# One of VectorE's score rows computed by GpSimd in 84 of 128 attention blocks

## The chip, the core and the metric

The kernel runs on one core of a Trainium2 chip. The metric is the device time of one execution in microseconds (us). Of the engines, PE is TensorE, DVE is VectorE, ACT is ScalarE, POOL is GpSimd and SP is the queue that issues the transfers.

## What is computed

Eight graphs of 2048 nodes with 128 features go through four layers. Each layer is a residual sum and a layer norm. Layers 0, 2 and 3 multiply by a normalised adjacency matrix and a weight. Layer 1 is an attention whose score is not a plain product:

```python
# layers 0, 2, 3 (with small differences in the degree)
x = layernorm(x + (D^-1/2 (adj + I) D^-1/2 x) W + b)
# layer 1, per graph, i and j over 2048 nodes, d over 128 features
q = x @ WQ
k = x @ WK
h = relu(q[:, None, :, :] + k[:, :, None, :])
score = einsum('bijd,d->bij', h, p)
att = softmax(score + mask)           # mask: 0 where adj > 0, else -1e22
x = layernorm(x + att @ x)
```

The array `h` has 2048 x 2048 x 128 elements for each graph, and making it is most of the work.

## The kernel before

**Blocks and rows.** The attention of a graph is cut into 16 blocks (`t` from 0 to 15) of 128 nodes i; eight graphs give 128 blocks. In a block the 128 nodes are walked as 32 groups (`g`) of 4 rows (`u`). One row is one instruction over a 128 x 2048 tile (features by nodes j) for one node i: it takes `q` and the column of `k` that belongs to i. Of the 32 groups, 20 are DVE's (kind "D", L990, a max of two packed half-precision numbers read as one float) and 12 are ACT's (kind "A", L756, a relu). The groups g = 2, 5, 7, 10, 13, 15, 18, 21, 23, 26, 29, 31 are ACT's.

**Rings.** The rows of a group lie in `big`. Each kind has a ring of two groups (`RING = 2`), so DVE may write its group number r only when PE has used up group r - 2 (`rows_used["D"]`). In one block DVE's groups are g = 0, 1, 3, 4, 6, and so on, so group 4 goes into the place of group 1, and group 3 into that of group 0.

**PE.** For each group PE runs `score_rows` (L1134): it multiplies the rows by a window of weights, 32 matmuls for a D group, into the four banks of `score`. It takes the groups in the order of g, whoever made them. Between groups it does its other work (`side`): transposes of adjacency tiles (L1034), products of the graph layers (L1057, L1075), the attention product (L1116).

**Side work.** The layers 0, 2 and 3 of other graphs run beside the attention, each in four steps. Step s of layer2 has its block 2 + s, of layer3 its block 6 + s, of layer0 its block 10 + s (`BLOCK`). Every engine walks the same list of places (32 for a block), and `side` says what stands at a place. The sum of a step (`sum_layer`, place 35 of its step) falls on g = 3 of the block behind: DVE runs four products with sum that read PSUM (L871), four BN_STATS (L877) and four BN_AGGR (L883), and after that its rows of g = 3. POOL's `layer_root` (L587, L589) stands at g = 4, and `norm_layer` (L890), which uses its result, at g = 8. The sums fall on blocks 3 to 14; the first attention has layer0 alone (4 sums), six have all twelve, the last one has eight: 84 blocks in all. Twelve more sums lie outside the attention.

**Softmax.** The scores of the block before are read by DVE (`masked_scores`, L941, L945) between row u = 1 and row u = 2 of g = 1 (in block 0 at g = 0).

**Order.** All of it is written out by hand: each engine's instructions stand in program order, with semaphores between the engines. `load_k` and `load_q` on SP bring the columns of `k` and the tiles of `q` for later rows and wait until the rows that read the old ones are done.

Of the kernel before, what the change touches and what calls it, by code (L numbers as in the profile page):

```python
# [9 lines left out]
ALU = mybir.AluOpType  # L10
# [20 lines left out]
def build(nc, x, adj, w0, b0, wq, wk, p, w2, b2, w3, b3, out):  # L31
# [50 lines left out]
    with ExitStack() as ctx:  # L82
# [3 lines left out]
        def sem(name):  # L86
            return ctx.enter_context(nc.semaphore(name))
# [134 lines left out]
        att_variance_ready = sem("att_variance_ready")  # L222
        att_rstd_ready = sem("att_rstd_ready")
        att_output = sem("att_output")

        block = ctx.enter_context(nc.Block())

# [5 lines left out]

        def masked_at(t):
            return (0, 0) if t == 0 else (1, 2)

# [3 lines left out]
        def one_of(c, *which):  # L242
            return c in which

        def block_of(c, t):
            return c * T + (T + t)
# [8 lines left out]
        def step_of(c, name, s):  # L255
            return layer_of(c, name) * STEPS + s
# [104 lines left out]
        def _(sp):  # L361
# [43 lines left out]
            def load_k(c, t):  # L405
                sp.wait_ge(k_stored, qk_step(c + 1, t // PER) * 16 + 16)
                sp.wait_ge(pair_stored, split_of(c + 1, t // PER, 1) * 16 + 16)
                n = block_of(c, t)
                if not one_of(c, FIRST) or t > 1:
                    for kind in "AD":  # L410
                        sp.wait_ge(rows_ready[kind], (c * T + (T + t - 1)) * N_OF[kind])
                sp.dma_start(k_cols[:, t % 2, :], k_kept[n]).then_inc(k_loaded[t % 2], 16)
                sp.dma_start(k_pair_cols[:, t % 2, :], k_pair_kept[n]).then_inc(k_loaded[t % 2], 16)

# [103 lines left out]
            def load_q(c):  # L518
                sp.wait_ge(q_stored, qk_step(c + 1, STEPS) * 16)
                sp.wait_ge(pair_stored, split_of(c + 1, STEPS, 0) * 16)  # L520
                if not one_of(c, FIRST):
                    sp.wait_ge(rows_ready["A"], (c + 1) * (T * N_OF["A"]))
                sp.dma_start(q_f32[:], q_kept[c + 1]).then_inc(q_loaded, 16)
                if not one_of(c, FIRST):
                    sp.wait_ge(rows_ready["D"], (c + 1) * (T * N_OF["D"]))
                sp.dma_start(q_pair[:], q_pair_kept[c + 1]).then_inc(q_pair_loaded, 16)

            def attention(c):
# [45 lines left out]
        @block.gpsimd  # L574
        def _(pool):
            pool.memset(ident[:], 0.0).then_inc(ident_cleared, 1)
            pool.wait_ge(ident_cleared, 1)
            pool.affine_select(out=ident[:], in_=ident[:], compare_op=ALU.not_equal, fill=1.0, base=0,
                               pattern=[[-1, P]], channel_multiplier=1).then_inc(ident_ready, 1)
            pool.wait_ge(minus_half_ready, 1)  # L580
            pool.wait_ge(bound_ready, 2)
            pool.tensor_tensor(bound, bound2, plus_half, ALU.pow).then_inc(bound_ready, 1)

            def layer_root(c, name, s):
                n = step_of(c, name, s) + 1
                pool.wait_ge(moments_ready, n)
                pool.tensor_scalar(var_eps[:], moments[:, :, 1], EPS, None, ALU.add).then_inc(variance_ready, 1)  # L587
                pool.wait_ge(variance_ready, n)
                pool.tensor_tensor(rstd[:], var_eps[:], minus_half[:, 0:PER], ALU.pow).then_inc(rstd_ready, 1)  # L589

            def att_root(m):
                pool.wait_ge(att_moments_ready, m + 1)
                pool.tensor_scalar(att_var[:], att_mom[:, 1:2], EPS, None, ALU.add).then_inc(att_variance_ready, 1)  # L593
                pool.wait_ge(att_variance_ready, m + 1)
                pool.tensor_tensor(att_rstd[:], att_var[:], minus_half[:, 0:1], ALU.pow).then_inc(att_rstd_ready, 1)

            def hold_roots(c):
                pool.wait_ge(roots_ready, roots_before(c))
                pool.tensor_copy(dis_hold[:], dis_new[:, 1:3, :]).then_inc(roots_ready, 1)

            def degree_roots(c):
                pool.wait_ge(degrees_ready, c + 3)
                if not one_of(c, OPENING):
                    pool.wait_ge(roots_ready, roots_before(c) + 1)
                for i in range(3):
                    pool.tensor_tensor(dis_new[:, i, :], deg_sum[:, i, :], minus_half[:], ALU.pow).then_inc(roots_ready, 1)

            def keep_roots(c):
                pool.wait_ge(roots_ready, roots_before(c) + (1 if one_of(c, LAST) else 4))
                pool.tensor_copy(dis_use[:], dis_hold[:]).then_inc(roots_ready, 1)  # L610

            def side(c, place):
                for name, s in steps_at(c, place, ROOT_AT):
                    layer_root(c, name, s)
                if place == DIS_AT:
                    if not one_of(c, OPENING, CLOSING):
                        hold_roots(c)
                    if not one_of(c, LAST, CLOSING):
                        degree_roots(c)
                if place == KEEP_AT and not one_of(c, OPENING, CLOSING):  # L620
                    keep_roots(c)

            def attention(c):
                for place in range(PLACES):
                    t, g = divmod(place, GROUPS)
                    if g == NORM_AT and (t > 0 or not one_of(c, FIRST)):
                        att_root(c * T + (T + t - 1))
                    side(c, place)

            for place in range(PLACES):  # L630
                side(OPENING, place)
            attention(FIRST)
            for c in range(B - 2):
                attention(c)
            attention(LAST)
            att_root(B * T - 1)
            for place in range(PLACES):
                side(CLOSING, place)
# [137 lines left out]
        def _(dve):  # L776
# [88 lines left out]
            def sum_layer(c, name, s):  # L865
                n = step_of(c, name, s) + 1
                dve.wait_ge(biased, n)
                dve.wait_ge(layer_projected, n)
                for j in range(PER):
                    t = s * PER + j  # L870
                    ins = nc.vector.scalar_tensor_tensor(out=gx[:, t, :], in0=acc[0][:, j * P:(j + 1) * P],  # L871
                                                         scalar=dis[name][:, t:t + 1], in1=gx[:, t, :],
                                                         op0=ALU.mult, op1=ALU.add)
                ins.then_inc(layer_summed, 1)
                dve.wait_ge(layer_summed, n)
                for j in range(PER):
                    ins = nc.vector.bn_stats(stats[:, j, :], gx[:, s * PER + j, :])  # L877
                ins.then_inc(stats_ready, 1)
                dve.wait_ge(stats_ready, n)
                if n > 1:  # L880
                    dve.wait_ge(layer_output, n - 1)
                for j in range(PER):
                    ins = nc.vector.bn_aggr(moments[:, j, :], stats[:, j, :])  # L883
                ins.then_inc(moments_ready, 1)
# [81 lines left out]
            def attention(c):  # L966
                for place in range(PLACES):
# [12 lines left out]
                    if KIND[g] == "D":  # L980
                        if RANK[g] == 0:
                            if t == 0:
                                dve.wait_ge(q_pair_loaded, (c + 2) * 16)
                            dve.wait_ge(k_loaded[t % 2], (c + 1) * (T // 2 * 32) + (t // 2 * 32 + 32))
                        dve.wait_ge(rows_used["D"], n * N_OF["D"] + (RANK[g] + 1))
                        for u in range(P // QUAD):
                            if before and u > 0 and (g, u) == masked_at(t):
                                masked_scores(n)

                            ins = nc.vector.tensor_scalar(ring["D"][:, RANK[g] % RING * 4 + u, :], q_pair[:],  # L990
                                                          k_pair_cols[:, t % 2, QUAD * u + g:QUAD * u + g + 1],
                                                          None, ALU.max)
                        ins.then_inc(rows_ready["D"], 1)
# [17 lines left out]
        def _(pe):  # L1011
# [106 lines left out]
                if cc == CHUNKS - 1:  # L1118
                    ins.then_inc(acc_full, 1)

            def score_rows(n, g):
                kind = KIND[g]
                pe.wait_ge(rows_ready[kind], n * N_OF[kind] + (RANK[g] + 1))
                window = unit_window if kind == "D" else sign_window
                for cc in range(CHUNKS):
# [17 lines left out]
            def attention(c):  # L1143
                for place in range(PLACES):
# [9 lines left out]
                            pe.wait_ge(x1_ready, (c + 2) * 16)  # L1154
                        weigh(m, MULTIPLY_AT[g], steps_turned(c, place))
                    side(c, place)
                    score_rows(block_of(c, t), g)

            for u in range(UNITS):
                first_unit(u)  # L1160
# [41 lines left out]
```

## Time and profile before

| what | value |
|---|---|
| median of 3 runs | 14251.69 us (14249.84 to 14259.41) |
| the profiled execution, its own time | 14255.09 us |
| its span, first to last instruction | 14253.3 us |
| PE busy | 13023.6 us (91%) |
| DVE busy | 13509.2 us (95%) |
| ACT busy | 13092.2 us (92%) |
| POOL busy | 668.9 us (5%) |
| mean granted TensorE clock | 0.982 of full speed |

Three engines are nearly full, and POOL is nearly empty. A busy share is an average: which engine holds up the others changes several times within a block, so the place of the change has to be read in the order of time. The granted clock has two levels here, full (2.4 GHz) and half (1.2 GHz).

### The profile page before, as it was taken

What the parts mean: (1) busy time and instruction counts of PE and PEld (TensorE: products, weight loads), DVE (VectorE), ACT (ScalarE), POOL (GpSimd) and SP (SyncE); (2) the same over time, 40 slices, a digit from 0 to 9 for tenths busy, and PEclk for the clock granted to TensorE, in tenths of its full rate; (3) what the DMA queues carried; (4) which work ended last, traced back from release to release, by engine and by line L of the source; (5) the groups of instructions that cost most, each with busy time, mean ns of one, the idle gap of its engine ahead of it and who ended that gap; (6) DMA issues with size and microseconds to landing.
All of it is one profiled execution on the core that took longest, in us unless ns stands there. A gap on an engine that the chain in (4) does not pass through costs nothing.

```text
span 14253.3 us, 317325 instructions
## 1 busy us (share of the span) xinstructions
PE 13023.6 (91%) x143877; PEld 5459.3 (38%) x143877; DVE 13509.2 (95%) x14168; ACT 13092.2 (92%) x8612; POOL 668.9 (5%) x495
## 2 busy tenths in 40 slices
PE   6889989999899988999989998899989999899988
PEld 3333334443344333443334433344333433333333
DVE  5999999999999999999999999999999999999995
ACT  5999899998999899998999989999899998998994
POOL 0000000000000000000000000000000000000000
PEclk7999999999999999999999999999999999999999
DMA  5111112221122111221122211222112221011103
GB/s 184 45 51 47 49 52 86 85 61 50 55 86 87 62 40 63 87 87 56 36 72 84 86 56 36 75 84 85 56 35 75 88 78 56 30 49 51 42 12 108
DMA packets 714328, 935.44 MB, mean 66 GB/s; under 512 B 61713, under 2 KB 455953, under 8 KB 693521
## 3 DMA queue, kind: packets, MB, share of 16 engines
q1 hardware_dynamic: 712976, 915.13, 20.5%
q8 instruction: 1128, 18.48, 0.5%
q14 instruction: 224, 1.83, 0.0%
HBM read 722.01 MB, written 184.55 MB: 64 GB/s over the span
## 4 chain that ended last, share of the span: by engine, by line
PE 45%; DVE 35%; ACT 16%; issue 2%; DMA 2%; SPq 0%; POOL 0%; ACTq 0%; DVEq 0%; POOLq 0%
PE score L1134 33%; DVE big L990 31%; ACT big L756 14%; PE acc L1057 6%; PE turn L1034 2%; PE acc L1116 2%; DVE att L941 2%; DVE gx L871 1%; DMA piece<-adj_turned 1%; DMA big<-in_adj_dram 0%; ACT y_turned L679 0%; DVE stats L877 0%; ACT turned L669 0%; DMA q_pair_kept<-turned 0%; PE acc L1075 0%
## 5 line engine op out<-in xcount | busy, mean ns | idle before, releaser
L990 DVE TENSOR_SCALAR big<-q_pair,k_pair_cols 128x2048 f32<-128x2048 f32 x10240 | 12366.6, 1281 | 380.0 <-PE score L1134 362.6
L756 ACT ACTIVATE big<-q_f,k_cols 128x2048 f32<-128x2048 f32 x6144 | 11746.9, 1999 | 70.2 <-DMA q_f<-q_kept 44.1
L1134 PE MATMUL score<-big,unit_window 128*32 128x512 f16 x81920 | 5178.8, 396 | 819.0 <-DVE big L990 788.4
L1134 PE MATMUL score<-big,sign_window 128*32 128x512 f32 x49152 | 5619.7, 597 | 273.2 <-ACT big L756 268.6
L1134 PEld LDWEIGHTS score<-big,unit_window 128*32 128x32 bf16 x81920 | 2270.4, 96 | 4003.1 <-DVE big L990 1242.9
L1134 PEld LDWEIGHTS score<-big,sign_window 128*32 128x32 f32 x49152 | 1569.0, 110 | 3603.8 <-issue 3005.9
L1057 PE MATMUL acc<-piece,gs 128*128 128x512 f32 x3072 | 1446.6, 598 | 36.0 <-DMA piece<-adj_turned 23.6
L1057 PEld LDWEIGHTS acc<-piece,gs 128*128 128x128 f32 x3072 | 533.8, 191 | 545.4 <-issue 459.1
L737 ACT ACTIVATE att_turned<-turn 128x512 f32<-128x512 f32 x512 | 300.9, 588 | 390.5 <-PE turn L1034 389.7
L593 POOL TENSOR_SCALAR att_var<-att_mom 128x1 f32<-128x1 f32 x128 | 66.0, 515 | 10641.0 <-DVE att_mom L959 10641.0
L1116 PE MATMUL acc<-x,att_turned 128*128 128x128 f32 x4096 | 554.9, 279 | 0.0
L693 ACT ACTIVATE y_turned<-acc 128x512 f32<-128x512 f32 x96 | 57.7, 601 | 523.4 <-PE acc L1057 522.8
L1116 PEld LDWEIGHTS acc<-x,att_turned 128*128 128x128 f32 x4096 | 498.3, 192 | 56.8 <-issue 56.8
L941 DVE CUSTOM_DVE_ANT_0 att<-score,att 128x512 f32<-128x512 f32 x512 | 324.7, 687 | 42.1 <-PE score L1134 41.6
L1034 PEld LDWEIGHTS turn<-ident,att 128*128 128x128 f32 x2048 | 215.2, 141 | 331.9 <-issue 327.0
L1034 PE MATMUL turn<-ident,att 128*128 128x128 f32 x2048 | 336.5, 287 | 3.8 <-ACT att L733 3.1
L1034 PE MATMUL turn<-ident,raw 128*128 128x128 f32 x1792 | 277.0, 277 | 29.0 <-DMA raw<-in_adj_dram 29.0
L669 ACT ACTIVATE turned<-turn 128x512 f32<-128x512 f32 x448 | 262.1, 585 | 34.4 <-PE turn L1034 34.4
L733 ACT ACTIVATE att<-att,neg_max 128x2048 f32<-128x2048 f32 x128 | 256.0, 2000 | 20.4 <-DVE neg_max L945 19.9
L1034 PEld LDWEIGHTS turn<-ident,raw 128*128 128x128 f32 x1792 | 203.9, 141 | 120.1 <-issue 84.1
L682 ACT ACTIVATE y_turned<-raw 128x1024 bf16<-128x1024 f32 x224 | 237.1, 1058 | 7.1
L587 POOL TENSOR_SCALAR var_eps<-moments 128x4 f32<-128x4 f32 x96 | 110.6, 1152 | 2699.7 <-DVE moments L883 2699.7
(88 smaller groups left out, 2592.0 us busy)
## 6 DMA issues: line engine op xcount, KB each, us to landing
piece<-adj_turned SPq DMA_DIRECT2D x1536, 256.0 KB, 2.8
att<-in_adj_dram SPq DMA_DIRECT2D x128, 1024.0 KB, 5.1
raw<-in_adj_dram SPq DMA_DIRECT2D x224, 512.0 KB, 4.6
adj_turned<-turned SPq DMA_DIRECT2D x224, 512.0 KB, 4.3
big<-in_adj_dram SPq DMA_DIRECT2D x32, 512.0 KB, 7.6
adj_turned<-big SPq DMA_DIRECT2D x32, 512.0 KB, 6.9
gx<-in_x_dram SPq DMA_DIRECT2D x32, 256.0 KB, 4.2
q_kept<-raw SPq DMA_DIRECT2D x32, 256.0 KB, 3.4
```

Source lines behind the costliest of these rows:

```text
L669: nc.scalar.activation(stage[:, k * BANK:(k + 1) * BANK], turn[1][:], ACT.Copy).then_inc(turn_free[1], 1)
L682: nc.scalar.activation(unread, raw[:], ACT.Abs, accum_out=abs_part[:, u % 2, u // 2:u // 2 + 1]).then_inc(raw_abs_summed, 1)
L733: nc.scalar.activation(att[:], att[:], ACT.Exp, bias=neg_max[:], accum_out=row_sum[:]).then_inc(exp_ready, 1)
L737: nc.scalar.activation(att_turned[:, cc % 2, :], turn[0][:], ACT.Copy).then_inc(turn_free[0], 1)
L756: ins = nc.scalar.activation(ring["A"][:, RANK[g] % RING * 4 + u, :], q_f32[:], ACT.Relu, bias=k_cols[:, t % 2, QUAD * u + g:QUAD * u + g ...
L871: ins = nc.vector.scalar_tensor_tensor(out=gx[:, t, :], in0=acc[0][:, j * P:(j + 1) * P], scalar=dis[name][:, t:t + 1], in1=gx[:, t, :], o ...
L941: nc.vector.tensor_tensor_reduce(out=part, in0=score[:, cc, :], in1=part, scale=1.0, scalar=-3.0e38, op0=ALU.add, op1=ALU.max, accum_out=b ...
L990: ins = nc.vector.tensor_scalar(ring["D"][:, RANK[g] % RING * 4 + u, :], q_pair[:], k_pair_cols[:, t % 2, QUAD * u + g:QUAD * u + g + 1], ...
L1034: ins = nc.tensor.transpose(turn[k][:, j * P:(j + 1) * P], src(j), ident[:])
L1057: nc.tensor.matmul(acc[1][:], gs[:, i, :], piece[:, i % PIECES, :], start=(i == 0), stop=(i == T - 1)) \
L1116: ins = nc.tensor.matmul(acc[0][:, 0:D], att_turned[:, cc % 2, j * P:(j + 1) * P], x1[:, cc * PER + j, :], start=(cc == 0 and j == 0), sto ...
L1134: ins = nc.tensor.matmul(score[QUAD * u:QUAD * (u + 1), cc, :], window[:, QUAD - 1 - g:2 * QUAD - 1 - g], row, start=(g == 0 and part == 0 ...
```

## The change

In each of the 84 blocks, row u = 3 of group g = 4 is taken from DVE's list and put on POOL's. POOL computes it with an instruction of two operations: a min with 3.0e38, which alters no value that occurs, and then the same max. POOL waits for four things: a new semaphore `pool_may_go`, which the first of the four products of that sum raises; `q` and `k` in place; and `rows_used["D"]`, the same count that DVE waits for before its own rows of g = 4. In POOL's order the row stands ahead of `layer_root` of the same sum. PE waits in `score_rows` for `pool_row_ready` beside `rows_ready`, and SP's `load_k` and `load_q` wait for it too.

```diff
+        POOL_ROW = (4, 3)
+
+        def sums_at(c, t):
+            return [(name, s) for name in side_layers(c) for s in range(STEPS) if BLOCK[name] + s + 1 == t]
+
+        def has_pool_row(c, t):
+            return len(sums_at(c, t)) > 0
+
+        def pool_rows(c, t):
+            return sum(has_pool_row(a, k) for a in range(FIRST, c + 1) for k in range(T) if a < c or k < t)
...
@@ load_k, SP
+                    done = pool_rows(c, t - 1) if t > 0 else pool_rows(c - 1, T - 1)
+                    if done > 0:
+                        sp.wait_ge(pool_row_ready, done)
...
@@ load_q, SP
+                    sp.wait_ge(pool_row_ready, pool_rows(c, 0))
...
@@ POOL
+            def row(c, t):
+                g, u = POOL_ROW
+                n = block_of(c, t)
+                for name, s in sums_at(c, t):
+                    pool.wait_ge(pool_may_go, step_of(c, name, s) + 1)
+                pool.wait_ge(q_pair_loaded, (c + 2) * 16)
+                pool.wait_ge(k_loaded[t % 2], (c + 1) * (T // 2 * 32) + (t // 2 * 32 + 32))
+                pool.wait_ge(rows_used["D"], n * N_OF["D"] + (RANK[g] + 1))
+                pool.tensor_scalar(ring["D"][:, RANK[g] % RING * 4 + u, :], q_pair[:], 3.0e38,
+                                   k_pair_cols[:, t % 2, QUAD * u + g:QUAD * u + g + 1], ALU.min, ALU.max) \
+                    .then_inc(pool_row_ready, 1)
...
+                    if g == POOL_ROW[0] and has_pool_row(c, t):
+                        row(c, t)
...
@@ sum_layer, DVE
                 for j in range(PER):
                     t = s * PER + j
+                    if j == 1:
+                        ins.then_inc(pool_may_go, 1)
...
@@ attention, DVE
+                            if (g, u) == POOL_ROW and has_pool_row(c, t):
+                                continue
...
@@ PE
-            def score_rows(n, g):
-                kind = KIND[g]
+            def score_rows(c, t, g):
+                kind, n = KIND[g], block_of(c, t)
+                if g == POOL_ROW[0] and has_pool_row(c, t):
+                    pe.wait_ge(pool_row_ready, pool_rows(c, t) + 1)
                 pe.wait_ge(rows_ready[kind], n * N_OF[kind] + (RANK[g] + 1))
```

The rows of DVE's program around one such sum, in the kernel before. L871, L877 and L883 are the sum, L990 a row of scores, L890 the norm of the step.

```order
L945 TENSOR_REDUCE neg_max<-bank_max 128x1 [waits scores_read]
L990 TENSOR_SCALAR big<-q_pair,k_pair_cols 128x2048 x2
L871 SCALAR_TENSOR_TENSOR gx<-acc,dis_use,gx 128x128 [waits layer_projected,biased]
L871 SCALAR_TENSOR_TENSOR gx<-acc,dis_use,gx 128x128 x3
L877 BN_STATS stats<-gx 128x6 [waits layer_summed]
L877 BN_STATS stats<-gx 128x6 x3
L883 BN_AGGR moments<-stats 128x2 [waits layer_output,stats_ready]
L883 BN_AGGR moments<-stats 128x2 x3
L990 TENSOR_SCALAR big<-q_pair,k_pair_cols 128x2048 [waits vector_rows_used]
L990 TENSOR_SCALAR big<-q_pair,k_pair_cols 128x2048 x3
L990 TENSOR_SCALAR big<-q_pair,k_pair_cols 128x2048 [waits vector_rows_used]
L990 TENSOR_SCALAR big<-q_pair,k_pair_cols 128x2048 x3
```

The same place in the changed kernel, where L905, L911 and L917 are the sum and L1026 a row of scores.

```order
L905 SCALAR_TENSOR_TENSOR gx<-acc,dis_use,gx 128x128 [waits layer_projected,biased]
L905 SCALAR_TENSOR_TENSOR gx<-acc,dis_use,gx 128x128 x3
L911 BN_STATS stats<-gx 128x6 [waits layer_summed]
L911 BN_STATS stats<-gx 128x6 x3
L917 BN_AGGR moments<-stats 128x2 [waits layer_output,stats_ready]
L917 BN_AGGR moments<-stats 128x2 x3
L1026 TENSOR_SCALAR big<-q_pair,k_pair_cols 128x2048 [waits vector_rows_used]
L1026 TENSOR_SCALAR big<-q_pair,k_pair_cols 128x2048 x3
L1026 TENSOR_SCALAR big<-q_pair,k_pair_cols 128x2048 [waits vector_rows_used]
L1026 TENSOR_SCALAR big<-q_pair,k_pair_cols 128x2048 x2
```

Group g = 3 keeps its four rows, and group g = 4 has three. POOL's program there, in the changed kernel: L623 is the row, L605 and L607 the root of the step (L587 and L589 before), L611 and L613 the root of the attention.

```order
L613 TENSOR_TENSOR att_rstd<-att_var,minus_half 128x1 [waits att_variance_ready]
L623 TENSOR_SCALAR big<-q_pair,k_pair_cols 128x2048 [waits k1_loaded,vector_rows_used,q_pair_loaded,pool_may_go]
L605 TENSOR_SCALAR var_eps<-moments 128x4 [waits moments_ready]
L607 TENSOR_TENSOR rstd<-var_eps,minus_half 128x4 [waits variance_ready]
L611 TENSOR_SCALAR att_var<-att_mom 128x1 [waits att_moments_ready]
```

The row stands between the two roots, and it is the only instruction that POOL gains in a block.

## Rows read from the trace of the kernel before

**Rows 1.** The page: busy time of each engine, and the chain that ended last.

```profile
PE 13023.6 (91%) x143877; PEld 5459.3 (38%) x143877; DVE 13509.2 (95%) x14168; ACT 13092.2 (92%) x8612; POOL 668.9 (5%) x495
...
PE 45%; DVE 35%; ACT 16%; issue 2%; DMA 2%; SPq 0%; POOL 0%; ACTq 0%; DVEq 0%; POOLq 0%
```

**Rows 2.** The chain around one sum: start us, us, what.

```profile
5974.18 2.47 DVE big L990 x2
5976.65 1.05 DVE gx L871 x4
...
5978.63 0.38 DVE moments L883 x4
5979.01 9.55 DVE big L990 x8
5988.56 0.04 issue
5988.60 5.42 PE score L1134 x55
```

**Rows 3.** DVE in time there: start us, us, engine line op, operands, count.

```profile
5976.57 1.12 DVE L871 SCALAR_TENSOR_TENSOR gx<-acc,dis_use,gx 128x128 f32<-128x128 f32 x4
5977.72 0.87 DVE L877 BATCH_NORM_STATS2 stats<-gx 128x6 f32<-128x128 f32 x4
5978.63 0.38 DVE L883 BATCH_NORM_AGGREGATE moments<-stats 128x2 f32<-128x6 f32 x4
5978.93 14.41 DVE L990 TENSOR_SCALAR big<-q_pair,k_pair_cols 128x2048 f32<-128x2048 f32 x12
```

**Rows 4.** PE in time there: the groups 0 and 1, 2, 3 and 4.

```profile
5975.62 3.82 PE L1134 MATMUL score<-big,unit_window 128*32 128x512 f16 x64
5979.26 3.62 PE L1134 MATMUL score<-big,sign_window 128*32 128x512 f32 x32
5983.82 2.00 PE L1134 MATMUL score<-big,unit_window 128*32 128x512 f16 x32 [0.95 <-DVE big L990]
5988.60 1.99 PE L1134 MATMUL score<-big,unit_window 128*32 128x512 f16 x32 [2.78 <-DVE big L990]
```

**Rows 5.** PE in time, another such block: groups 1, 2, 3 and 4.

```profile
5115.80 2.02 PE L1134 MATMUL score<-big,unit_window 128*32 128x512 f16 x32 [1.95 <-DVE big L990]
5117.63 3.62 PE L1134 MATMUL score<-big,sign_window 128*32 128x512 f32 x32
5122.91 1.99 PE L1134 MATMUL score<-big,unit_window 128*32 128x512 f16 x32 [1.66 <-DVE big L990]
```

**Rows 6.** DVE's rows by their line: duration ns min/median/max.

```profile
L990 DVE TENSOR_SCALAR big<-q_pair,k_pair_cols x10240: 1251/1281/1307, 235.8 to 14065.5; 128x2048 f32<-128x2048 f32 x197
```

**Rows 7.** POOL in time: beside DVE's rows, and where DVE has none.

```profile
5979.10 1.18 POOL L587 TENSOR_SCALAR var_eps<-moments 128x4 f32<-128x4 f32 x1 [29.47 <-DVE moments L883]
5980.35 2.26 POOL L589 TENSOR_TENSOR rstd<-var_eps,minus_half 128x4 f32<-128x4 f32 x1
...
165.70 0.23 POOL L587 TENSOR_SCALAR var_eps<-moments 128x4 f32<-128x4 f32 x1 [28.18 <-DVE moments L883]
166.01 1.03 POOL L589 TENSOR_TENSOR rstd<-var_eps,minus_half 128x4 f32<-128x4 f32 x1
```

**Rows 8.** POOL by line and form: busy us, mean ns of one, idle before.

```profile
L578 POOL TENSOR_SCALAR_AFFINE_SELECT ident<-ident 128x128 f32<-128x128 f32 x1 | 0.3, 294 | 0.2 <-POOL ident L576 0.2
L576 POOL MEMSET ident<- 128x128 f32 x1 | 0.2, 206 | 0.3 <-POOLq L1189 0.3
L1189 POOL MEMSET const-float32-1.0<- 128x1 f32 x1 | 0.1, 100 | 0.0
```

**Rows 9.** TensorE's clock (PEclk, behind POOL) behind the idle time, two blocks.

```profile
4465.30:4468.70 3.40, 3.28 (x32) 1.27 (x36) 3.40 (x4) 3.40 (x2) 0.00 (x0) 0.50 0.00 0
6207.40:6210.80 3.40, 3.28 (x48) 1.40 (x52) 3.40 (x4) 3.40 (x2) 0.00 (x0) 1.00 0.00 0
```

**Rows 10.** PE's group 4 at half clock (first, last, and the block of rows 9), and at full.

```profile
1416.47 3.01 PE L1134 MATMUL score<-big,unit_window 128*32 128x512 f16 x32 [2.79 <-DVE big L990]
...
4465.42 3.51 PE L1134 MATMUL score<-big,unit_window 128*32 128x512 f16 x32 [2.78 <-DVE big L990]
...
6207.52 2.00 PE L1134 MATMUL score<-big,unit_window 128*32 128x512 f16 x32 [2.78 <-DVE big L990]
...
13373.62 3.24 PE L1134 MATMUL score<-big,unit_window 128*32 128x512 f16 x32 [2.80 <-DVE big L990]
```

**Rows 11.** The first product of this and of the next sum, for the same two blocks.

```profile
4453.38 1.12 DVE L871 SCALAR_TENSOR_TENSOR gx<-acc,dis_use,gx 128x128 f32<-128x128 f32 x4
...
4563.53 1.12 DVE L871 SCALAR_TENSOR_TENSOR gx<-acc,dis_use,gx 128x128 f32<-128x128 f32 x4
...
6195.49 1.12 DVE L871 SCALAR_TENSOR_TENSOR gx<-acc,dis_use,gx 128x128 f32<-128x128 f32 x4
...
6304.25 1.12 DVE L871 SCALAR_TENSOR_TENSOR gx<-acc,dis_use,gx 128x128 f32<-128x128 f32 x4
```

More of the change, by code:

```diff
@@ L224, in build @@
         att_output = sem("att_output")
+        pool_row_ready = sem("pool_row_ready")
+        pool_may_go = sem("pool_may_go")
         block = ctx.enter_context(nc.Block())
@@ L1156, in attention @@
                     side(c, place)
-                    score_rows(block_of(c, t), g)
+                    score_rows(c, t, g)
             for u in range(UNITS):
```

## Prediction, made before the changed kernel was run

> **What bounds the kernel now.** I read the page first, then the chain of waits around one sum, then the timelines of DVE, PE and POOL there, and last the granted clock. The page shows three engines above 90% and POOL at 5%, and a chain that is PE for 45%, DVE for 35% and ACT for 16% [rows 1]. So the bound changes hands within a block, and only the chain tells who holds it at the place of the change. There it is DVE, without a break: the last two rows of group 1, the sum, then eight rows (groups 3 and 4), and then PE takes over with group 4 [rows 2]. PE stands idle 0.95 us before group 3 and 2.78 us before group 4, both times for DVE [rows 4]. The pattern is the same in all 84 blocks with a sum: the first product of the sum is on the chain, DVE's rows begin 2.36 us behind its start, and PE begins group 4 at 12.04 us (5976.57 to 5988.60 in [rows 3, 4]). So a microsecond that DVE gains or loses between the sum and group 4 moves PE's group 4, and the chain goes on from there.
>
> **What the change removes.** One row of the eight. Rows follow each other every (14.41 - 1.28) / 11 = 1.19 us [rows 3, 6]. 84 x 1.19 = 100 us come off the chain, if nothing comes on.
>
> **When POOL's row can begin.** The words of the change say behind the first product, which is 0.3 us into the sum. But the row goes into the ring place of group 1, and POOL also waits until PE has used that group. PE is not that far. In the block of [rows 4] groups 0 and 1 end at 5979.44, which is 2.87 us behind the start of the sum. In the block of [rows 5], where PE is early, group 1 ends at 5117.82, with the sum begun 7.25 us before PE's group 3 at 5122.91, hence at 5115.66: 2.16 us. I find the early kind in 35 of the 84 blocks (2.14 to 2.20 us) and the late kind in 49 (2.4 to 2.96 us). DVE begins its rows at 2.36 us. So the cover of the sum is gone when POOL gets the go: in the early kind POOL starts about 0.09 us behind PE (the delay of var_eps behind the last BN_AGGR: 5979.01 to 5979.10 in [rows 2, 7]), just ahead of DVE, and in the late kind DVE's first row is already running.
>
> **What happens when the two meet.** POOL's small instructions show one side. var_eps takes 0.23 us alone and 1.18 us when it is issued in the middle of a DVE row; it ends with that row. The root takes 1.03 us alone and 2.26 us beside rows [rows 7]. So POOL waits for the row that runs, and gets in between two rows although DVE has the next one ready. DVE shows nothing of it: its longest row in 10240 is 1307 ns [rows 6]. But these POOL instructions touch 1 to 16 elements a partition. No row of this trace has a long POOL instruction, so what DVE pays must be bounded. I take the same exclusion to hold in the other direction: DVE's next row waits for POOL's whole row.
>
> The Trainium skill says so too ("SBUF — State Buffer", Who interferes with whom): whichever of a DVE instruction in a two-port mode and a GpSimd instruction comes first holds the shared ports for its whole length and the other blocks fully, and tensor_scalar can be in such a mode while a product that reads PSUM is not. The trace agrees for POOL's side (0.23 against 1.18 us); no row of it shows DVE's side. By that rule the place behind the first product would be right, if the ring let POOL use it.
>
> **How long POOL's row takes.** Alone, a POOL tensor_scalar of 4 elements takes 0.23 us [rows 7]. The slope per element is bounded by the two instructions that have 128 elements: memset, (206 - 100) / 127 = 0.83 ns, and affine_select, at most (294 - 100) / 128 = 1.5 ns [rows 8]. With 2048 elements the row is 0.2 + 1.7 = 1.9 us or 0.2 + 3.1 = 3.3 us. I take the lower slope: an estimate from memset's row, since affine_select has its own fixed cost in its 294 ns. In the early kind DVE loses 2.16 + 0.09 + 1.9 - 2.36 = 1.8 us; in the late kind the fixed part lies beside DVE's first row and DVE loses 1.7 us and two hand-overs of about 0.1 us. I take 1.9 us for both. Bounds: 0 (DVE isn't held at all) and 3.3 us.
>
> "GPSIMD Engine Reference", 3.1, of the Trainium skill gives 1.03 cycles an element at 1.2 GHz for bodies of up to two operations, which would be an estimate of 1.76 us for the elements; no run here shows it yet.
>
> **The term of DVE's path.** (1.9 - 1.19) x 84 = 60 us slower. The bounds make it -100 and (3.3 - 1.19) x 84 = +177 us.
>
> **TensorE's clock.** Behind the 2.78 us of idle time before group 4 the granted clock is at its lower level (1.2 GHz) in some blocks: 0.50 for 3.4 us in the block at 4465 and 1.00 in the one at 6207 [rows 9]. Group 4 then takes 3.51 us where it takes 2.00 us [rows 10]. By the duration of group 4 this is so in 42 of the 84 blocks (first and last in [rows 10]). None of the 84 has a slow group 3, which has 0.9 to 1.7 us of idle time before it [rows 4, 5]. What it costs a block is the time to the next sum: 110.15 us against 108.76 us [rows 11], 1.4 us; other pairs that I compared lie between 0 and 1.5 us, so I take 1.0, and 42 us in all.
> The change shifts the idle time. Group 3 is ready later by what DVE loses, 1.9 us: PE waits 2.8 to 3.6 us before group 3. Group 4 follows three rows later, 3.6 us, of which PE works 2.0: it waits 1.6 us there. A wait of up to 1.7 us was never followed by the lower clock, so I expect the low stretches to move to group 3. There they cost little, since a group 3 of 3.5 us (as group 4 in [rows 10]) still ends before group 4's rows are ready at 3.6 us. I leave 12 us for stretches that reach into group 4. The term is 12 - 42 = -30 us, with bounds -50 (all of the cost gone) and +42 (both places slow).
>
> **Other parts.** POOL's roots come later by about 3 us; rstd ends at 5982.61 [rows 7], and the norm stands behind the twelve rows of DVE that last to 5993.3 [rows 3], so 0. PE's added wait holds up only group 4, and POOL is done some 5 us before DVE's third row of it: 0; if POOL came later than that, everything behind it in PE's order would wait. SP waits for rows that are done a block earlier: 0.
>
> **Sum.** 60 - 30 = +30 us on the profiled execution's 14255.1 us. That execution is 3.4 us above the median of the runs shown, and I put the difference on the median: 14251.7 + 30 = 14282 us. A change under 0.2% (28 us) can't be told from none in a measurement of this kernel, so this forecast lies just beyond that.
>
> **Rivals.**
> - *Faster: DVE is not held.* POOL reads and writes between DVE's accesses, or DVE is held only a little. For it: DVE's rows don't lengthen beside POOL's small instructions [rows 6, 7]. Against it: POOL is held by DVE, so something is shared. DVE gains 1.19 x 84 = 100 us; PE's wait before group 4 falls to 1.6 us, so the 42 us of the clock go too. ACT at 92% would take some of it back. 14252 - 100 - 42 = 14110 us at best; 14130 to 14200 where DVE is held for half a row. It decides below 0.9 us of loss. Chance 0.22.
> - *No change: the loss is 1.5 to 1.9 us and the clock gives back 45 us or more.* Memset's slope without hand-overs gives 1.7: (1.7 - 1.19) x 84 = 43 us, less 45. 14250 us, up to 14275. Chance 0.28.
> - *Much slower: POOL's row has affine_select's slope.* 3.3 us: 14252 + 177 - 42 + 12 = 14399 us. Two operations instead of one and a scalar read from memory speak for it; that affine_select builds a pattern as well speaks against it. Chance 0.12.
> - *Starved: POOL doesn't get in until DVE's run of rows ends.* In [rows 3] the run is 14.41 us long; PE would wait for the row from 12 to about 19 us, some 7 us in each of 84 blocks, 590 us. var_eps, which gets in within 1.18 us, speaks against it. Chance 0.03.
>
> **How the numbers follow.** My forecast (slower by 28 to 90 us) has 0.35; with the two slower rivals (0.12 and 0.03) the chance of slower is 0.50, of no change 0.28, of faster 0.22. The forecast's own range is 14262 to 14340 us. For 8 in 10 I go down to 14185, where half a row's hold still lies, and up to 14390, near affine_select's slope; the full gain and the starved case stay outside.
>
> **What would show it.** In the changed kernel POOL's row (L623) should start 2.2 to 2.3 us behind the first product in some blocks and 2.5 to 3.0 us in the others, never at 0.4. DVE should show a hole or one long row of 1.7 to 2.0 us in g = 3. PE's wait before group 3 should be 2.8 us or more and before group 4 about 1.6 us, with the lower clock at group 3 and full clock at group 4. POOL's row should be done in 1.9 to 3 us. The prediction is wrong if DVE's rows keep their 1.19 us beside POOL's row, if the row lasts over 2.5 us, or if the lower clock comes as often at group 4 as before.

## The result, and the profile after

| kernel | median us | runs | against the kernel before, with its 95% interval |
|---|---|---|---|
| before | 14252.8 | 11 | |
| changed | 14295.4 | 11 | 1.0035 [1.0019, 1.0051] |

The change costs 42.6 us. One of its eleven runs took 14409.0 us at a mean granted clock of 0.944, where the others had 0.976 to 0.979; without it the median is 14291.1 us. The profiled execution of the changed kernel took 14306.2 us, 11 us above its median, so single blocks are compared below rather than the two spans.

The page of the changed kernel, engines first and then its chain. DVE is busier by 35 us although it has 84 instructions less, and POOL by 298 us (compare [rows 1]).

```profile
PE 13055.2 (91%) x143877; PEld 5481.5 (38%) x143877; DVE 13544.5 (95%) x14084; ACT 13092.1 (92%) x8612; POOL 967.3 (7%) x579
...
PE 42%; DVE 35%; ACT 18%; issue 2%; DMA 2%; SPq 0%; POOL 0%; ACTq 0%; DVEq 0%; POOLq 0%
```

The chain around the sum of the same block as in [rows 2] (start us, us, what).

```profile
5988.81 2.47 DVE big L1026 x2
5991.28 1.05 DVE gx L905 x4
...
5993.26 0.38 DVE moments L917 x4
5993.64 10.00 DVE big L1026 x7
6003.63 0.14 issue
6003.77 5.45 PE score L1172 x62
```

Seven rows take 10.00 us where eight took 9.55 us, and PE starts 0.14 us behind the last of them instead of 0.04 us, now that it waits for two semaphores there. In the mean of the 84 blocks PE's group 4 begins 12.57 us behind the sum's start; it was 12.04 us.

POOL in time there.

```profile
5994.31 3.44 POOL L623 TENSOR_SCALAR big<-q_pair,k_pair_cols 128x2048 f32<-128x2048 f32 x1 [30.05 <-PE score L1172]
5997.73 1.20 POOL L605 TENSOR_SCALAR var_eps<-moments 128x4 f32<-128x4 f32 x1
5999.01 2.26 POOL L607 TENSOR_TENSOR rstd<-var_eps,minus_half 128x4 f32<-128x4 f32 x1
```

What released the row is PE's score, not DVE's product, and the row starts 3.12 us behind the sum's start (5991.19). The DVE row that was running at 5997 us, and the line's extremes (min/median/max in ns; compare [rows 6]):

```profile
5995.92 2.92 DVE L1026 TENSOR_SCALAR big<-q_pair,k_pair_cols 128x2048 f32<-128x2048 f32 x1
...
L1026 DVE TENSOR_SCALAR big<-q_pair,k_pair_cols x10156: 1251/1280/2926, 237.2 to 14117.5; 128x2048 f32<-128x2048 f32 x200
```

One row, the third of group 3, lasts 2.92 instead of 1.28 us. The 1.64 us more are what POOL's row costs DVE; below they are called the hold. Each of the 84 blocks has one such row of 2.91 to 2.93 us: the third of group 3 in 82 blocks, the fourth in two.

PE in time (groups 0 and 1, 2, 3, 4), which answers to [rows 4].

```profile
5990.25 3.85 PE L1172 MATMUL score<-big,unit_window 128*32 128x512 f16 x64
5993.91 3.63 PE L1172 MATMUL score<-big,sign_window 128*32 128x512 f32 x32
6000.09 2.00 PE L1172 MATMUL score<-big,unit_window 128*32 128x512 f16 x32 [2.55 <-DVE big L1026]
6003.77 2.01 PE L1172 MATMUL score<-big,unit_window 128*32 128x512 f16 x32 [1.68 <-DVE big L1026]
```

PE now waits 2.55 us before group 3 (0.95 before) and 1.68 us before group 4 (2.78 before).

### The profile page after: what moved, and what is told of

Its sections match the earlier page's. It is cut to its first block, busy times and chain, and to the rows that moved or that the text cites. A ratio compares the mean times of both kernels' runs of the same rounds, so it can differ in the third digit from the quotient of the medians.

```text
span 14304.4 us, 317584 instructions
## 1 busy us (share of the span) xinstructions
PE 13055.2 (91%) x143877; PEld 5481.5 (38%) x143877; DVE 13544.5 (95%) x14084; ACT 13092.1 (92%) x8612; POOL 967.3 (7%) x579
## 4 chain that ended last, share of the span: by engine, by line
PE 42%; DVE 35%; ACT 18%; issue 2%; DMA 2%; SPq 0%; POOL 0%; ACTq 0%; DVEq 0%; POOLq 0%
DVE big L1026 31%; PE score L1172 31%; ACT big L788 16%; PE acc L1093 6%; PE turn L1070 2%; PE acc L1152 2%; DVE att L975 2%; DVE gx L905 1%; DMA piece<-adj_turned 1%; ACT y_turned L711 0%; ACT turned L701 0%; DMA q_pair_kept<-turned 0%; DVE stats L911 0%; DMA big<-in_adj_dram 0%; PE acc L1111 0%
## 5 line engine op out<-in xcount | busy, mean ns | idle before, releaser
L1026 DVE TENSOR_SCALAR big<-q_pair,k_pair_cols 128x2048 f32<-128x2048 f32 x10156 | 12401.1, 1293 | 394.6 <-PE score L1172 373.5
L611 POOL TENSOR_SCALAR att_var<-att_mom 128x1 f32<-128x1 f32 x128 | 65.3, 511 | 10379.2 <-DVE att_mom L993 10379.2
L623 POOL TENSOR_SCALAR big<-q_pair,k_pair_cols 128x2048 f32<-128x2048 f32 x84 | 311.5, 3708 | 2488.8 <-PE score L1172 2488.8
```

Source lines behind the costliest of these rows:

```text
L623: pool.tensor_scalar(ring["D"][:, RANK[g] % RING * 4 + u, :], q_pair[:], 3.0e38, k_pair_cols[:, t % 2, QUAD * u + g:QUAD * u + g + 1], ALU ...
```

## Experiments

Each kernel is the changed one with the edit shown, if nothing else is said. The cover is work of DVE beside which POOL's row can run without holding DVE; early and late blocks are those of the prediction (35 and 49 of the 84). Every median stands beside runs of the kernel before on the same chip (14254.7 to 14257.2 us).

**Where the row lies.**

```diff
-        POOL_ROW = (4, 3)
+        POOL_ROW = (3, 3)
```

> POOL's row is moved from (g 4, u 3) to (g 3, u 3), with the same wait on the first product; its ring place is that of group 0, which PE has used up 0.1 to 0.9 us behind the start of the sum. Theory A (the ring count of group 1 let POOL start only when the cover of the sum was gone, and DVE then stands still for POOL's elements): POOL starts 0.4 to 1.0 us behind the first product, its 1.7 us of elements lie mostly beside the sum, DVE's hole of 1.64 us shrinks to 0 to 0.6 us, PE's group 3 and 4 come 0.6 to 1.2 us earlier than in the kernel before; 14252 - 84 x 0.6 to 1.2 = 14150 to 14200 us. Rival B (a POOL row costs DVE its full length wherever it lies, through something else than rows of DVE): hole stays near 1.6 us and the time near 14290 us.

14204.8 us, ratio 0.9962 [0.9950, 0.9975]: 52 us faster than before, 91 us faster than the changed kernel. POOL and the DVE row beside it, in the same block (the sum starts at 5955.49):

```profile
5956.77 1.99 POOL L623 TENSOR_SCALAR big<-q_pair,k_pair_cols 128x2048 f32<-128x2048 f32 x1 [28.21 <-PE score L1172]
...
5957.84 1.99 DVE L1026 TENSOR_SCALAR big<-q_pair,k_pair_cols 128x2048 f32<-128x2048 f32 x1
```

POOL starts at 1.28 us and runs 1.99 us without a break. DVE's first row is held until it ends, 0.7 us instead of 1.64. In the early blocks POOL runs from 0.46 to 2.44 us, and DVE isn't held at all. Even here the first product was the last wait in 35 blocks only, the ring in 49. Theory A's mechanism stands, and rival B is out. The time is 5 us above theory A's range. PE's group 4 begins 0.84 us earlier than in the kernel before, 71 us in all, of which 52 arrive. From one sum to the next, the early blocks of the profiled execution are 1.2 us shorter and the late ones 0.3 us, where their group 4 is 0.6 us earlier; what takes up the rest there was not traced.

**Is it the new semaphore?**

```diff
-                for name, s in sums_at(c, t):
-                    pool.wait_ge(pool_may_go, step_of(c, name, s) + 1)
```

> The changed kernel without the wait on the first product; the row (4, 3) waits for the ring count and its inputs alone. Theory A: the ring count comes last in all 84 blocks, so nothing changes: POOL's row starts 2.3 to 3.9 us behind the first product and the time is that of the changed kernel, 14285 to 14305 us. Rival C (the new semaphore is what holds POOL): POOL starts earlier by up to 1 us and the time moves by more than 20 us.

14293.7 us (changed: 14295.4). POOL starts at 2.4 to 3.9 us, as in the changed kernel. The wait on the first product does nothing at (4, 3).

**The most that could be had.** DVE and POOL both leave the row out, with POOL's call and the waits on `pool_row_ready` taken away.

> The row (4, 3) of the 84 blocks is computed by nobody (PE reads what the ring place holds); DVE has one row less and POOL none more. This gives the most that the change could bring. Theory A: PE's group 4 begins at 10.84 instead of 12.04 us behind the sum's start, 84 x 1.19 = 100 us less; and with PE's wait before group 4 down from 2.78 to 1.6 us the lower granted clock at group 4 goes, 42 us more if it cost what I took: 14110 us, 14150 us without the clock's part. Rival D (the path isn't DVE's behind group 4, ACT or PE take most of it back): 14200 us or more.

14128.1 us, ratio 0.9909: 129 us less. PE's groups 3 and 4 in the same block:

```profile
5936.95 1.99 PE L1164 MATMUL score<-big,unit_window 128*32 128x512 f16 x32 [0.94 <-DVE big L1020]
5940.54 2.00 PE L1164 MATMUL score<-big,unit_window 128*32 128x512 f16 x32 [1.60 <-DVE big L1020]
```

Group 4 starts 10.84 us behind the sum (5929.70), as worked out. No group 4 of the 84 runs at the lower clock, and the gain is 29 us more than the rows' 100, where the expectation had 42. Rival D is out: the path gives the whole gain through.

**How the hold grows with the row.**

```diff
-                pool.tensor_scalar(ring["D"][:, RANK[g] % RING * 4 + u, :], q_pair[:], 3.0e38,
+                pool.tensor_scalar(ring["D"][:, RANK[g] % RING * 4 + u, 0:N // 2], q_pair[:, 0:N // 2], 3.0e38,
```

> POOL's row has 1024 elements instead of 2048, the other half is computed by nobody. Theory A (DVE is held for POOL's elements at 0.84 ns each): the hole in DVE's rows is 1.64 - 0.86 = 0.8 us, POOL's row ends at about 5.7 instead of 6.56 us behind the sum's start, PE's group 4 at 11.7; 14290 - 84 x 0.86 = 14220 us. Rival E (the hole is a fixed price of the hand-over): hole 1.6 us, 14290 us.

14216.1 us, ratio 0.9971. The held DVE row:

```profile
5964.84 2.06 DVE L1026 TENSOR_SCALAR big<-q_pair,k_pair_cols 128x2048 f32<-128x2048 f32 x1
```

2.06 - 1.28 = 0.78 us for 1024 elements against 1.64 us for 2048: 0.84 ns for each element more, and no fixed part is left. The hold grows with POOL's elements. Rival E is out.

**What POOL's first access is.**

```diff
-                                   k_pair_cols[:, t % 2, QUAD * u + g:QUAD * u + g + 1], ALU.min, ALU.max) \
+                                   0.0, ALU.min, ALU.max) \
```

> The changed kernel with 0.0 as an immediate in POOL's row instead of the column of k (that row of the output's scores is then another one). In the changed kernel POOL's row never gets in at the first boundary of DVE's rows behind its issue, but at the second (issued at 2.4 to 3.5 us it ends at 6.56 us, issued at 3.7 us or later at 7.76 us). Theory F: its first access is the 128 x 1 column, which takes the first boundary, and the elements need the next. Then without the column POOL's elements run at the first boundary: POOL ends at about 5.4 us where it is issued before 3.5 us, and DVE's hole lies between its second and third row of group 3. Rival G: the set-up of any long POOL instruction costs that boundary: ends stay at 6.56 us. Both: hole 1.64 us, time near 14290 us.

One run, 14287.5 us. POOL and the held DVE row (the sum starts at 5983.47):

```profile
5986.56 2.27 POOL L623 TENSOR_SCALAR big<-q_pair 128x2048 f32<-128x2048 f32 x1 [30.02 <-PE score L1171]
...
5987.00 2.92 DVE L1025 TENSOR_SCALAR big<-q_pair,k_pair_cols 128x2048 f32<-128x2048 f32 x1
```

Issued at 3.09 us, POOL ends at 5.36 instead of 6.56 us, one DVE row earlier, and the held row is the second of group 3 instead of the third. Over the 84 blocks POOL ends at 5.4 us in 69, at 4.2 in 10 and at 6.6 in 5, where the changed kernel has 6.6 in 82 and 7.8 in two. Rival G is out and theory F stands: without the column of k POOL's row needs one gap between DVE's rows less. That the column itself is read in that gap is the plain reading; no record shows the read by itself. The hold is the same 1.64 us.

**Does the min cost time?**

```diff
-                pool.tensor_scalar(..., q_pair[:], 3.0e38,
-                                   k_pair_cols[...], ALU.min, ALU.max) \
+                pool.tensor_scalar(..., q_pair[:],
+                                   k_pair_cols[...], None, ALU.max) \
```

> POOL's row with the max alone instead of min and max. Theory A (bound by moving the elements, 0.84 ns each): the same 1.64 us hole, the same ends at 6.56 us, 14285 to 14305 us. Rival H (the second operation costs time): the hole shrinks by 0.3 us or more, 14270 us or less.

One run, 14577.3 us, and neither A nor H. POOL's row and the held DVE row:

```profile
6093.77 6.87 POOL L623 TENSOR_SCALAR big<-q_pair,k_pair_cols 128x2048 f32<-128x2048 f32 x1 [30.10 <-PE score L1172]
...
6095.33 6.39 DVE L1026 TENSOR_SCALAR big<-q_pair,k_pair_cols 128x2048 f32<-128x2048 f32 x1
```

With the max alone DVE is held 6.39 - 1.28 = 5.11 us, 2.5 ns an element: three times as slow as with both operations. All 84 blocks show it (held rows of 6.39 to 6.42 us), so it doesn't hang on the one run. The min is no burden; the form with both operations is the faster one on POOL. Why, these runs don't show.

**Another cover: the reads of the scores.** `MASK_ROW` is a row of POOL at these reads, `SUM_ROW` one at the sum. DVE reads `score` in PSUM for 2.6 us in every block but the first of all, in 120 of them between u = 1 and u = 2 of group 1.

```diff
+        SUM_ROW, MASK_ROW = None, (1, 3)
+            return ([MASK_ROW] if MASK_ROW and t > 0 else []) + ([SUM_ROW] if SUM_ROW and sums_at(c, t) else [])
...
+                if (g, u) == MASK_ROW:
+                    pool.wait_ge(scores_read, n * CHUNKS + 1)
```

> No row of POOL at the sum. Instead POOL computes row (g 1, u 3) in every block but the first of a graph (120 blocks), started behind the first of the four reads of the scores (masked_scores), 2.6 us of work in which DVE reads PSUM; its ring place is free by then, as PE used up the last groups of the block before ahead of those reads. Theory A (a POOL row costs DVE only what sticks out of work that reads PSUM; its length alone is 1.98 us): POOL runs from 0.7 to 2.7 us behind the first read, DVE is held for 0.1 us or less, and one row of 1.19 us is saved in 120 blocks: 143 us at most, of which I expect 80 to 140, since in blocks without a sum PE is nearer to the bound: 14115 to 14175 us. Rival B (a POOL row costs DVE its length wherever it lies): 14252 + 120 x 0.5 = 14310 us.

14185.3 us, ratio 0.9950 [0.9937, 0.9962]. The cover holds: POOL starts at 5948.98 us, 0.79 us behind DVE's first read, and ends with DVE's next row not delayed. All 120 rows have a mean of 1.97 us.

```profile
L625 POOL TENSOR_SCALAR big<-q_pair,k_pair_cols 128x2048 f32<-128x2048 f32 x120 | 236.8, 1974 | 2735.6 <-DVE bank_max L978 2735.6
```

But the gain is 70 us, not 80 to 140. In this kernel 62 instead of 42 of the 84 groups 4 run at the lower clock, which is part of the gap. By the profiled executions, the 35 early blocks are 38 us shorter in all, nearly a whole row each; the 49 late ones are 18 us shorter and the blocks without a sum 14 us, a third of a row each. What takes the gain back there was not traced.

**Both rows.** `SUM_ROW, MASK_ROW = (3, 3), (1, 3)`.

> The row (1, 3) behind the first read of the scores in 120 blocks and the row (3, 3) behind the first product of the sum in 84. Theory A: the second row needs PE to have used group 0, and in the 49 blocks of the late kind that falls 0.9 us behind the sum's start; with the sum 1.2 us earlier it falls at 2.1 us, so POOL starts there only when the cover is over and DVE is held for up to 1.7 us. In the early kind both rows are free. So less than the sum of both alone (52 us for (3, 3)): 14252 - 110 - 10 to 50, 14090 to 14140 us. If the two add up fully, about 14065 us.

14158.6 us, ratio 0.9933 [0.9920, 0.9947], 18 us above the range of the expectation. In a late block the two rows of POOL are

```profile
5935.41 1.97 POOL L625 TENSOR_SCALAR big<-q_pair,k_pair_cols 128x2048 f32<-128x2048 f32 x1 [22.70 <-DVE bank_max L978]
5940.90 4.09 POOL L625 TENSOR_SCALAR big<-q_pair,k_pair_cols 128x2048 f32<-128x2048 f32 x1 [3.53 <-PE score L1176]
```

The second is issued 2.46 us behind the sum's start (5938.44), 0.1 us behind DVE's first row, and shows the waits and the hold of the changed kernel.

**Only where PE is early.** The kernel with both rows, with this edit:

```diff
-... ([SUM_ROW] if SUM_ROW and sums_at(c, t) else [])
+... ([SUM_ROW] if SUM_ROW and sums_at(c, t) and t in (6, 10, 12, 13, 14) else [])
```

> Row (1, 3) in 120 blocks as in e7, and row (3, 3) only in the 35 blocks (t = 6, 10, 12, 13, 14) where PE has used up group 0 near the start of the sum. In e8 the row (3, 3) of the other 49 blocks was issued behind the sum and held DVE for 1.64 us. Theory A: those 49 holes go and DVE computes that row itself in 1.19 us, 49 x 0.45 = 22 us less than e8: 14158 - 22 = 14137 us. Rival (the holes of e8 were off the path): 14150 to 14165 us.

14144.2 us, ratio 0.9924 [0.9910, 0.9938]: 14 us less than with all 84. Right in sign, short of the 22, and between theory A (14137) and the rival (14150 or more). PE's group 4 begins 0.24 us earlier in the mean, 20 us in all, but 58 instead of 51 of the groups 4 run at the lower clock, and 13 of the 35 blocks still hold DVE, since with the row at the scores the sum begins 1.2 us earlier against PE.

**The clock by itself.** The kernel before, with PE's idle time filled:

```diff
+                    if g == 4 and sums_at(c, t):
+                        pe.wait_ge(turn_free[0], weight_use(m, 0) + AHEAD)
+                        for j in range(12):
+                            nc.tensor.matmul(turn[0][:, 0:P], ident[:], ident[:], start=True, stop=True)
```

> The kernel before with the same 12 matmuls of PE ahead of group 4 of the 84 blocks; DVE and POOL are unchanged. This prices the clock by itself. My prediction took 42 us for the low stretches at group 4. Leaving out the row brought 129 us where the row alone is 100 us, which says 28 us. Theory K: no slow group 4 (42 of 84 before), 14253 - 28 = 14225 us, 14210 with my 42 us. Rival L: 14245 us or more.

14232.2 us, ratio 0.9985 [0.9976, 0.9994]. PE in time:

```profile
5975.23 2.00 PE L1137 MATMUL score<-big,unit_window 128*32 128x512 f16 x32 [0.94 <-DVE big L993]
5977.17 2.94 PE L1163 MATMUL turn<-ident 128*128 128x128 f32 x24
5980.04 2.01 PE L1137 MATMUL score<-big,unit_window 128*32 128x512 f16 x32
```

The 12 matmuls (two records each) fill all of the wait, and group 4 starts 12.06 us behind the sum on average instead of 12.04. None of the 84 groups 4 is slow. The clock at group 4 cost 23 us, a little more than half of the 42 I had taken, and 7 us outside theory K's 14210 to 14225; rival L (14245 or more) is further off. PE's group 6 begins 0.74 us earlier than before in the mean of the 84 blocks, group 9 only 0.37 us: half of what the full clock saves at group 4 is gone by then.

The changed kernel with the same filling, 10 matmuls ahead of group 3 and 6 ahead of group 4:

> The changed kernel with PE's idle time filled by small matmuls (10 ahead of group 3, 6 ahead of group 4 in the 84 blocks). With the same done to the kernel before (14232 us) it gives DVE's part of the change without the clock's: PE's group 4 begins 12.57 instead of 12.04 us behind the sum's start, 84 x 0.53 = 45 us. Theory M (the clock gave back nothing: its low stretches cost about as much in the changed kernel as before, 20 us): 14295 - 20 = 14275 us, which is also 14232 + 45. Rival N (the clock did give back 30 us as I forecast and DVE's part is larger than 45 us): no more is left to gain, 14290 us or more, and the difference to 14232 us is 60 us or more.

14272.3 us, ratio 1.0011 [1.0002, 1.0020]. That is 23 us under the changed kernel and 40 us over the filled kernel before; with each ratio taken against its own runs of the kernel before, 27 and 38 us. None of the groups 3 and 4 of the 84 blocks is slow. Theory M stands: the clock costs 23 to 27 us in the changed kernel and 23 us before, and DVE's part is about 40 us (45 by the blocks). The intervals of the changed kernel and of this one are 23 and 13 us to either side, so the medians say that the two prices are alike, not that they are equal. That the clock still costs something in the changed kernel is clearer: all eleven runs here took 14267 to 14278 us, and none of the changed kernel's was under 14285 us.

**The fastest.** The kernel of the early blocks with 12 matmuls ahead of group 4:

> As e9, and PE fills 1.2 to 1.6 us of its idle time ahead of group 4 of the 84 blocks with 12 small matmuls (128 x 128 of the identity into a bank that is free then). Theory K (the lower granted clock at group 4 is caused by the 2.7 us of idle time and costs 20 to 40 us): group 4 takes 2.0 us in all 84 blocks and the time is 20 to 40 us below e9's. Rival L (the low stretches are off the path or come elsewhere instead): group 4 is at full clock and the time is within 10 us of e9's.

14087.4 us, ratio 0.9885 [0.9871, 0.9899]: 168 us (1.2%) under the kernel before, and 57 us under the same without the matmuls, more than I expected. With rows taken from DVE, 58 of the 84 groups 4 had run at the lower clock, now none, and the mean granted clock is 0.986 instead of 0.980.

## Why the prediction was right, and where not

The forecast was 14282 us, 30 us above the median before; measured are 43 us. The mechanism held: DVE is on the path from the sum to group 4, the ring lets POOL go only at the end of the sum, and DVE then stands still for POOL's row. The term of DVE's path was right in kind and too large, the term of the clock was wrong.

1. *What bounds the place.* Confirmed. Leaving the row out gave the full 100 us of DVE's rows and more.
2. *The start of POOL's row.* Confirmed: the ring count is the last wait, and without the semaphore nothing changes. I put the early kind "just ahead of DVE", at 2.25 us, with 0.09 us from PE's end to POOL's start. That delay is 0.21 to 0.24 us in all 84 blocks. So the earliest rows, 24 of them, start at 2.36 to 2.4 us, just behind the start of DVE's first row, and the others at 2.6 to 3.9 us: both kinds meet the same fate.
3. *The hand-over.* I let POOL in at the first boundary. It needs two while the scalar is the column of k, one with an immediate in its place, and DVE pays only for the last. In two blocks (t = 12 and 14) POOL is issued behind 3.6 us, and there the hold falls one row later.
4. *The size of the hold.* 1.64 us, where I took 1.9. Memset's slope of 0.83 ns was right (0.84 measured), and the row's 1.98 us alone too. What was wrong was to put the fixed part and the hand-overs on DVE. PE's second semaphore, which I had put at 0, costs 0.09 us: group 4 starts 0.147 us behind the end of DVE's last row in every one of the 84 blocks, where it was 0.055 us. The term is (1.64 - 1.19 + 0.09) x 84 = 45 us instead of 60.
5. *The clock: the step that failed.* I wrote 12 - 42 = -30 us. The price before was 23 us and not 42: I had taken it from a few pairs of blocks. And what was left was 23 to 27 us and not 12, so within what these runs resolve nothing came back: -23 + 23 = 0. The low stretches did move in part as forecast, from 42 slow groups 4 and no slow group 3 to 40 slow groups 3 and 20 slow groups 4. But "a wait of up to 1.7 us was never followed by the lower clock" doesn't carry over when group 3 itself is slow. All 20 slow groups 4 stand behind a slow group 3, after waits of 0.08 to 1.20 us, as in this block of the changed kernel:

```profile
4137.47 2.50 PE L1172 MATMUL score<-big,unit_window 128*32 128x512 f16 x32 [2.58 <-DVE big L1026]
4141.15 3.60 PE L1172 MATMUL score<-big,unit_window 128*32 128x512 f16 x32 [1.18 <-DVE big L1026]
```

```profile
4138.50:4141.90 3.40, 2.21 (x28) 0.66 (x21) 3.40 (x4) 3.40 (x2) 0.15 (x1) 0.54 0.00 0
4141.90:4145.30 3.40, 3.40 (x32) 1.29 (x28) 3.40 (x4) 3.40 (x3) 0.00 (x0) 0.50 0.00 0
```

   The clock (the number behind POOL's) is low at group 3 and still low at group 4, after only 1.18 us of waiting. The clock records of the whole execution agree: 115 low stretches of 641 us together in the changed kernel, 104 of 523 us before. The trace of the kernel before had the same pattern outside the 84 blocks, at groups 0 and 1 of the first block of five graphs, and I had looked at group 3 of the 84 alone:

```profile
5435.51 3.60 PE L1134 MATMUL score<-big,unit_window 128*32 128x512 f16 x32 [3.67 <-DVE big L990]
5440.29 3.60 PE L1134 MATMUL score<-big,unit_window 128*32 128x512 f16 x32 [1.18 <-DVE big L990]
```

So 45 + 0 = 45 us against the 43 measured; my 60 - 30 came near it in part by luck, with two errors of opposite sign.

One of the signs by which I had said that the prediction would be wrong did appear: POOL's row lasts over 2.5 us, 3.06 to 4.20 us in the 84 blocks. The sign was badly chosen. The record of the row takes in its waits for two gaps between DVE's rows, and the work in it is the 1.98 us of the row alone. Two more signs came out in part: PE waits 1.7 to 3.3 us before group 3, 2.75 in the mean, where I had 2.8 or more, and the clock is low at 20 groups 4, where I had full clock.

Of the rivals, *faster* fell with the held row of 2.92 us, *starved* with POOL's row of 3.44 us. *No change* had nearly the right loss for DVE (43 us), but wanted 45 us back from the clock. *Much slower* had the second operation against POOL, and it was the other way round: with a single operation the kernel took 322 us more than the one before.

## What to carry to other kernels

A row given to POOL is free only as long as DVE does work that doesn't need what POOL holds; so look for the last of all the waits that starts it, not for the one that the change adds. Here the cover was there, and the ring count of a different row, one group earlier, let POOL use all of it in 35 of the 84 blocks and part of it in the others. And when PE waits for another engine, read the granted clock behind the wait, and behind the next wait too: filling the wait with idle matmuls was worth 23 to 57 us here.

## What the runs showed of the hardware

- A GpSimd tensor_scalar over 2048 float elements with min and max took 1.98 us alone, and beside DVE's rows it held DVE for 0.84 ns an element (0.78 us for 1024 elements, 1.64 us for 2048); with max alone it held DVE for 2.5 ns an element (5.11 us).
- GpSimd gets in between two DVE rows that follow without a gap, and a DVE row that it holds is recorded as one long row (2.92 for 1.28 us). With a pointer scalar in place of an immediate it got in one such gap later (its end 6.56 instead of 5.36 us behind the sum's start).
- DVE's reduction that reads PSUM and one SBUF tensor leaves GpSimd's row at its full speed: 1.97 us over 120 rows. The Trainium skill ("SBUF — State Buffer", Who interferes with whom) says as much of instructions with at most one SBUF input outside the two-port modes, and these 120 rows agree. It says too that, where the two do contend, the one that comes second blocks fully; the held row agrees, with 1.64 us of standing still for POOL's row.
- A second semaphore in front of a PE instruction added 0.09 us to its start (0.147 instead of 0.055 us behind the end of DVE's last row, in all 84 blocks).
- The lower granted clock (1.2 GHz) lasted over a wait of PE of only 1.18 us where the group ahead of that wait had itself run at it.
